# Layer 0's output projection: 48 fp32 steps replaced by three products of rounded parts each

## What is computed

```python
x = L0_attn_hidden_states
x = _layernorm(x + _L0_attn_ref(x, ...), axis=-1)
x = _layernorm(x + _L0_ffn_ref(x, L0_ffn_gate_w, L0_ffn_gate_up_proj, L0_ffn_down_proj), axis=-1)
x = _layernorm(x + _L1_attn_ref(x, ...), axis=-1)
x = _layernorm(x + _L1_ffn_ref(x, L1_ffn_weight, L1_ffn_bias), axis=-1)
```

```python
scores = jnp.einsum('bqhd,bkhd->bhqk', qf, kf) * scale      # 16 heads, causal
p = jax.nn.softmax(scores, axis=-1)
o = jnp.einsum('bhqk,bkhd->bqhd', p, v)
o = o.reshape(B, T, H * D_V) @ Wo                            # the output projection
...
logits = jnp.matmul(x.astype(jnp.float32), gate_w.T.astype(jnp.float32))
p = jax.nn.sigmoid(logits)
w, idx = jax.lax.top_k(p / jnp.sum(p, axis=-1, keepdims=True), TOPK)   # 2 of 16 experts a token
```

## Time and profile before

| | us |
|---|---|
| median of 3 runs | 534.26 (533.25 to 538.05) |
| the profiled execution | 533.59 |
| its span in the trace | 531.1 |
| TensorE busy | 497.8 |
| VectorE, ScalarE, GpSimd busy | 380.4, 339.7, 294.0 |

### The profile page before, as it was taken

One profiled execution on the slowest core, in us unless ns is written; L12 is line 12 of the kernel. 1 busy time (PEld: TensorE's weight loads), 2 busy tenths in 40 slices (PEclk: granted clock), 3 DMA queues, 4 the chain that ended last, 5 costly groups with the idle time before them and its releaser, 6 DMA issues.

```text
span 531.1 us, 10729 instructions
## 1 busy us (share of the span) xinstructions
PE 497.8 (94%) x3592; PEld 434.7 (82%) x3592; DVE 380.4 (72%) x833; ACT 339.7 (64%) x761; POOL 294.0 (55%) x289
## 2 busy tenths in 40 slices
PE   8999999999999996899958979999999999999994
PEld 7668888888888785688836869999999999999883
DVE  4798888888883275655537897779857985588556
ACT  5756777777766646344324776778766876676663
POOL 5757677767764136255551676776554664465330
PEclk9999999999999999899987988999999999999998
DMA  8939999940000672455564000000000000000001
GB/s 270 398 85 383 314 331 318 322 151 0 0 1 1 225 295 81 114 156 162 181 216 171 0 1 2 1 0 2 1 2 1 1 2 0 2 1 1 0 22 60
DMA packets 17756, 56.78 MB, mean 107 GB/s; under 512 B 2628, under 2 KB 12362, under 8 KB 15914
## 3 DMA queue, kind: packets, MB, share of 16 engines
q1 hardware_dynamic: 14960, 49.81, 27.5%
q0 software_dynamic: 2752, 6.40, 3.6%
HBM read 49.19 MB, written 28.45 MB: 146 GB/s over the span
## 4 chain that ended last, share of the span: by engine, by line
PE 78%; DVE 7%; ACT 5%; issue 3%; DMA 3%; POOL 2%; SPq 0%; DVEq 0%; POOLq 0%; ACTq 0%
PE bank L443 10%; PE bank L445 10%; PE bank L444 10%; PE bank L991 5%; PE bank L586 5%; PE bank L508 4%; PE bank L611 3%; PE bank L1008 3%; PE bank L588 2%; PE bank L735 2%; PE bank L720 2%; PE bank L722 2%; PE bank L721 2%; PE bank L622 2%; PE bank L702 2%
## 5 line engine op out<-in xcount | busy, mean ns | idle before, releaser
L1100 ACT ACTIVATE probs<-bank,neg_max,q_scale 128x256 f32<-128x256 f32 (+1 forms) x128 | 63.7, 507 | 39.1 <-DVE neg_max L1770 39.1
L1986 POOL TENSOR_TENSOR probs<-probs,inv_sum 128x512 f32<-128x512 f32 x64 | 51.5, 826 | 44.1 <-DVE inv_sum L1778 44.1
L2019 POOL TENSOR_TENSOR exps<-exps,tables 128x256 f32<-128x256 f32 x32 | 24.7, 771 | 75.2 <-ACT exps L1210 75.0
L1210 ACT ACTIVATE exps<-bank 128x768 f32<-128x768 f32 x32 | 25.9, 808 | 41.3 <-PE bank L702 41.3
L1590 DVE TENSOR_TENSOR q_lo<-q_sum,q_hi 128x512 fp32r<-128x512 f32 x32 | 28.8, 899 | 29.0 <-ACT q_hi L1164 28.6
L2006 POOL TENSOR_TENSOR swapped<-swapped,tables 128x512 f32<-128x512 f32 x32 | 43.4, 1359 | 5.2 <-ACT swapped L1131 5.1
L2115 POOL DMA_INDIRECT y_rows<-y_slot,dest x31 | 29.7, 959 | 30.0 <-issue 18.2
L1756 DVE TENSOR_TENSOR swapped<-bank,tables 32x512 f32<-32x512 f32 x64 | 44.4, 693 | 1.4
L1978 POOL TENSOR_TENSOR qT<-qT,swapped 128x512 f32<-128x512 f32 x32 | 40.8, 1274 | 6.1 <-DVE swapped L1756 6.1
L443 PE MATMUL bank<-x,wq_hi 128*128 128x256 f32 x128 | 38.6, 301 | 0.1
L586 PE MATMUL bank<-keysT,qT 128*128 128x256 f32 x128 | 38.2, 380 | 0.0
(11 more groups left out here) (281 smaller groups left out, 1766.6 us busy)
## 6 DMA issues: line engine op xcount, KB each, us to landing
slots<-in_c_unused SPq DMA_DIRECT2D x20, 1036.0 KB, 35.5
gu_all<-in_gate_up SPq DMA_DIRECT2D x4, 1024.0 KB, 7.8
xg<-slots SPq DMA_DIRECT2D x31, 129.5 KB, 2.2
wvo_raw<-in_wvo SPq DMA_DIRECT2D x1, 2560.0 KB, 18.4
dn_all<-in_down SPq DMA_DIRECT2D x1, 2048.0 KB, 7.7
wq_full<-in_Wq SPq DMA_DIRECT2D x1, 2048.0 KB, 17.8
wo_raw<-in_Wo SPq DMA_DIRECT2D x1, 2048.0 KB
wqk_raw<-in_wqk SPq DMA_DIRECT2D x1, 1536.0 KB, 9.9
```

The source lines that it names most:

```text
L1100: ins = act.activation(probs[:, par, h, c0:c1], bank[:, 2 * par + h, c0:c1], ACT.Exp, bias=neg_max[:, par, i:i + 1], scale=q_scale[:, b, t ...
L1986: ins = pool.tensor_tensor(some, some, inv, ALU.mult)
```

## The change

Tiles 2 to 7 are made as three products of parts (144 fp32r matmuls for 48 fp32 ones); tiles 0 and 1 stay. For this the parts are made:

- ScalarE makes the high part of `wo_full` in two halves of 4 pairs (128x1024 each) at the end of units 28 and 29, and the high part of `ctxT0` for batches 1, 2 and 3, two halves each: batch 1 at the end of units 30 and 31, batch 2 at the end of step 32 and in `act_first_norm` behind the sigmoid's table load of b = 0, batch 3 in b = 1, one ahead of the root and one behind the sigmoid's table load. `ctx0_hi` has room for two batches, so batch 3 waits until tile 3 is made.
- VectorE makes the low part of the weights in units 30 and 31, behind the reciprocal.
- GpSimd makes the low parts of the context, in place of `ctxT0`: batch 1 in units 30 and 31 behind the normalisation, batches 2 and 3 behind the last unit, ahead of the DMA of `triangles`.
- TensorE waits for the low parts (`o0["w_lo"]`, `o0["ctx_lo"]`) ahead of steps 0 and 4 of each batch's first tile, and no longer for `ctx_copied`.
- A few semaphores are shared by two uses each, to make room for the three new ones; no wait moves by that.

```diff
     def pe_out0(eng, t, i):
 
-        mm = eng.matmul(out_bank0(t), ctxT0[:, i, t * P:t * P + P], wo_full[:, i, :],
-                        start=i == 0 and t != 1, stop=i == PAIRS - 1, skip_group_check=True)
+        if t < 2:
+            mm = eng.matmul(out_bank0(t), ctxT0[:, i, t * P:t * P + P], wo_full[:, i, :],
+                            start=i == 0 and t != 1, stop=i == PAIRS - 1, skip_group_check=True)
+        else:
+            b, c0 = t // 2, t % 2 * P
+            if t % 2 == 0 and i % 4 == 0:
+                eng.wait_ge(o0["ctx_lo"], 2 * (b - 1) + i // 4 + 1)
+            mm = three_pass(eng, out_bank0(t), ctx0_hi[:, b % 2, i, c0:c0 + P],
+                            ctx0_lo[:, i, t * P:t * P + P], wo0_hi[:, i, :], wo0_lo[:, i, :],
+                            i == 0, i == PAIRS - 1)
...
-            eng.wait_ge(at0["ctx_copied"], 4 * (PAIRS - 1) + b + 1)
+            if t == 2:
+                eng.wait_ge(o0["w_lo"], 2)
...
             load_table(act, 2 * b + 1, ACT.Sqrt)
+            if b == 1:
+                act_context0_hi(act, 3, 0)
             act.wait_ge(ln["var_ready"], 2 * b + 2)
...
             load_table(act, 2 * b + 2, ACT.Sigmoid)
+            if b < 2:
+                act_context0_hi(act, b + 2, 1)
...
+    def act_context0_hi(act, b, half):
+
+        act.wait_ge(at0["ctx_copied"], 4 * (4 * half + 3) + b + 1)
+        if b == 2 and half == 0:
+            act.wait_ge(at0["scores_done"], 4 * PAIRS)
+        if b == 3 and half == 0:
+            act.wait_ge(ln["y_done"], 4)
+        act.activation(ctx0_hi[:, b % 2, some_pairs(half), :], ctxT0[:, some_pairs(half), T * b:T * b + T],
+                       ACT.Copy).then_inc(o0["hi"], 1)
+
+    def context0_lo(eng, b, half):
+
+        eng.wait_ge(o0["hi"], 2 * b + half + 1)
+        some = slice(T * b, T * b + T)
+        eng.tensor_tensor(ctx0_lo[:, some_pairs(half), some], ctxT0[:, some_pairs(half), some], raw(ctx0_hi[:, b % 2, some_pairs(half), :]),
+                          ALU.subtract).then_inc(o0["ctx_lo"], 1)
...
+            if isinstance(n, int) and n >= 4 * PAIRS - 4:
+                if n < 4 * PAIRS - 2:
+                    act_weights_out0_hi(act, n - 4 * PAIRS + 4)
+                elif n < 4 * PAIRS:
+                    act_context0_hi(act, 1, n - 4 * PAIRS + 2)
+                elif n == 4 * PAIRS:
+                    act_context0_hi(act, 2, 0)
...
+            if isinstance(n, int) and 4 * PAIRS - 2 <= n < 4 * PAIRS:
+                half = n - 4 * PAIRS + 2
+                dve.wait_ge(o0["hi"], half + 1)
+                dve.wait_ge(at["q_done"], 4 * PAIRS)
+                dve.tensor_tensor(wo0_lo[:, some_pairs(half), :], wo_full[:, some_pairs(half), :],
+                                  raw(wo0_hi[:, some_pairs(half), :]), ALU.subtract).then_inc(o0["w_lo"], 1)
...
             if own and ahead(p, b, more):
                 pool_sin(pool, at, *ahead(p, b, more))
+            if isinstance(n, int) and 4 * PAIRS - 2 <= n < 4 * PAIRS:
+                context0_lo(pool, 1, n - 4 * PAIRS + 2)
 
         steps(pool, body)
+        for b in (2, 3):
+            for half in range(2):
+                context0_lo(pool, b, half)
```

More of the change, by code:

```diff
@@ L149, in build @@
     q_minus = sb("q_minus", [P, B, 2])
+    with ExitStack() as out_parts:
+        ctx0_hi = sb("ctx0_hi", [P, 2, PAIRS, T], F32R, out_parts)
     with ExitStack() as blocks:
@@ L215, in build @@
         wa_raw = sb("wa_raw", [P, KD, PROJ], F32, setup)
+    with ExitStack() as lows:
+        ctx0_lo = sb("ctx0_lo", [P, PAIRS, B * T], F32R, lows)
     with ExitStack() as layer0:
@@ L277, in build @@
     wk_hi, wk_lo = w_hi, w_lo
+    wo0_hi = wo_hi[:, PAIRS:H, :]
+    wo0_lo = latT_lo[:].rearrange("p k n -> p (k n)").rearrange("p (g d) -> p g d", d=D)
     slots = nc.dram_tensor("slots", (REGIONS * REGION, W), F32, kind="Internal").ap()
@@ L473, in pe_logits @@
         if b == 0:
[L474 removed]
+            eng.wait_ge(mo["ids_ready"], 2)
         else:
```

34 lines of the change are left out of this document (19 added, 15 removed).

## The result

The changed kernel took 546.47 us, the median of four executions (545.61 to 547.47). The kernel before, measured beside it, took 533.94 (four, 533.25 to 538.05). The ratio is 1.0221, with a 95% interval of 1.0184 to 1.0258: slower by 12.5 us. The forecast was 543.0 with a range of 538.5 to 547.0. So the sign and the range were right, and the point was 3.5 us too low. The profiled execution took 547.47 us, 13.9 more than the profiled one of before, over a span of 545.7 us for 531.1; it is the slowest of the four.

The account below looks back on a forecast made before the run. TensorE was taken as the bound, busy 497.8 of 531.1 us. Terms: +9.2 us at the first prefix product, +0.4 after it, 0 in the tail, +9.6, taken as +9.4 on 533.6: 543.0 us, range 538.5 to 547.

Parts of the forecast that it names:

- The products: Projection, tiles 2 to 7: three products take 0.36 us against 0.444 per step, gaining 4.0 us at most.
- The wait: First prefix product waits for the triangles DMA behind four GpSimd subtractions, starting at 197.5, 9.2 us late.
- The early clock: Pause of about 2 us before the first routing product: no clock loss in the forecast, 1.3 us in rival 2.
- rival 2: Longer wait for the table: landing 2.2 us slower, early clock 1.3 us, or more; 545 to 549 us, chance 0.09.
- The length of the wait: TensorE, there at 189.1, stands still some 8.5 us before the first prefix product.
- VectorE beside GpSimd: GpSimd's last normalisation, beside VectorE's weights subtractions, late by 0 to 1.4 us, taken as 0.7.
- GpSimd's subtraction: Each 128x1024 context low part on GpSimd takes 2.5 us; 2.3 or, if stretched, 3.4 possible.
- After the wait: First prefix product to batch 2's routing product: 2.0 us gained, 2.4 lost at half clock, +0.4.
- The tail: From batch 2's routing product to the experts: 0 us change; scatters start at about 198 without further cost.
- Rival 1: TensorE's clock stays up or returns at once after the wait for the table: 540.6 us, chance 0.14.
- Rival 3: Table is there when TensorE needs it, so not slower: 533.1 us, or 529.6 with all gains; chance 0.07.

Follow-up runs that it names:

- e2: Changed kernel with 16 unused small matmuls on TensorE in the pause before the first routing product: 545.44 us, ratio 1.0201.
- e1: Changed kernel with the triangles DMA issued ahead of GpSimd's low parts of batches 2 and 3: 538.93 us, ratio 1.0075.
- e3: Kernel before, no new products or parts, with only the triangles DMA issued late, behind a wait and two GpSimd subtractions: 545.13 us, ratio 1.0181.
- e4: Changed kernel with VectorE's second weights low part held until GpSimd's last normalisation is done: 544.59 us, ratio 1.0180.
- e5: Changed kernel with ScalarE's two copies of layer 1's weights moved behind the copies of x of batches 0 and 1: 542.03 us, ratio 1.0128.
- e8: As e7, but VectorE makes batch 3's context low parts and layer 1's second weights low part goes behind batch 1's slots: 534.87 us, ratio 0.9988.
- e6: Changed kernel with both edits, of e1 (table first) and e5 (copies moved): 535.12 us, ratio 0.9993.
- e7: As e6, with VectorE's weights parts ahead of the last two reciprocals and GpSimd's context low parts behind the last normalisation: 534.03 us, ratio 0.9984.
- e6_again: The kernel of e6 unchanged, run in a later session: 537.07 us, ratio 1.0040.
- e7_again: The kernel of e7 unchanged, run in a second session on the same chip as e8: 538.57 us, ratio 1.0056.
- e7_third: The kernel of e7 unchanged, run a third time: 537.12 us, ratio 1.0046.
- e8_again: The kernel of e8 unchanged, run once more: 534.80 us, ratio 1.0003.

## Why the prediction was right, and where it was off

**The products.** Right: three starts cover 0.36 us where one fp32 step took 0.444. The 4.0 us were worked out right and, as the prediction said, the part before the first prefix product only lengthened the wait.

**The wait.** Right in its mechanism, its place, its releaser and every link but one, VectorE's addition of batch 1, which waited for the slowed steps of tile 3 and not for the choice of experts. The table's DMA was issued at 196.50 (prediction: 194.4 + 0.7 = 195.1) and the prefix product started at 198.99 (197.5): 10.8 us later than before, 0.36 of it start-up, where +9.2 was forecast. The 1.5 us between 197.5 and 198.99 come apart into 0.36 for the start-up, 1.06 for the early clock, 0.2 for the last normalisation, -0.25 for GpSimd's last subtraction and +0.2 for the table's landing; 191.8 + 0.1 + 2.5 + 2.3 is 196.7 and not 196.8, which takes 0.1 off.

**The early clock.** This is the step that failed, though the range had room for it. The prediction let the first pause, forecast at 2 us and 1.85 in the profile, pass at the full clock, though its own row had a fall after 1.58 us; it stood only in rival 2, at 1.3 us. The clock went to 0.58 in the first 2 us after the pause. The routing product took 1.49 us for 0.95, and three steps of tile 3 took 0.64 us each for the 0.36 reckoned. It entered the path twice, by the routing product and by the 0.45 us that VectorE's addition waited for tile 3. So the root of batch 1 came at 191.38, 1.7 us later than the 189.0 + 0.7 forecast, start-up and late normalisation included. e2 measured the clock's part at 1.06 us.

**The length of the wait.** 6.26 us against 8.5. TensorE was there at 192.7 and not at 189.1, and that is mostly the clock: eight steps at 0.64 us and the late routing product. A shorter wait was no saving, since it ended later. Forecasting the end of the wait was worth more than forecasting its length.

**VectorE beside GpSimd.** Mis-sized: 0.7 us was taken from a range of 0 to 1.4. The last normalisation lasted 0.91 us longer; that it began 0.43 later (173.22 for 172.79) is the start-up, as it started right behind its reciprocal in both. Tile 2 began 1.25 us later than before, 0.89 of it from this. The Trainium skill ("SBUF — State Buffer", "Who interferes with whom") has whole-instruction exclusion, by which the prediction put the delay nearer to 1.2 than to 0.7. The trace agrees with the exclusion: the subtraction that started first, at 173.06, kept its 1.21 us, and the normalisation that came in at 173.22 was held. The size is 0.91, what was left of the subtraction and not the whole of it.

**GpSimd's subtraction.** 2.34 to 2.38 us for an estimate of 2.5; a little in the other direction, which hid some of the early clock by luck.

**After the wait.** Forecast +0.4 between the prefix product and the routing product of batch 2. Measured: 12.6 us (198.99 to 211.63) for 12.5 before, +0.2 with the rounding of both. Half rate lasted until 203.4, 4.4 us after the wait for the 4.8 reckoned, so it cost 2.2 us against the 2.0 gained, and the clock had fallen during the wait, not after it.

**The tail.** Forecast 0, measured +1.1 us: the experts' first product came 21.6 us after the routing product of batch 2 and 20.5 before. Most of it, 0.9 us, lies behind the last prefix product, before VectorE reads its result (222.30, idle 1.16 us there and 0.24 before). No run tells why, and it does not go with the change: e2 has this pause too (1.15 us), e1, e3, e4 and e5 do not (0.22 to 0.24). The scatters, forecast at about 198, started at 200.65; the prediction's own rows put them 2.4 us behind the prefix product, near 200, and it cost nothing.

Behind the experts' first product the distance was 12.1 us there and 13.2 where TensorE goes on after its wait of 7.5 us for `yg` (280.10 before, 293.28 now). Then the clock was granted at 0.50 for longer:

```profile
293.28 4.00 PE L507 MATMUL bank<-alibi_keys 128*128 128x256 bf16 x18 [7.53 <-DMA yg<-y_rows]
...
305.50:306.00 0.50, 0.50 (x5) 0.50 (x4) 0.31 (x1) 0.49 (x2) 0.00 (x0) 0.71 0.00 0
```

It was back at about 305.8, 12.5 us after work began, for 4.8 before, and by then the distance was 16.0 us; it shrank to 14.6 at the end. Of the other profiles only that of e8 has so late a return, the others take 4 to 5 us, so it is not shown to belong to the change. The profiled execution is the slowest of the four, which fits.

**The sum by its terms**, in the profiled executions: 10.8 at the prefix product (10.5 without the start-up), +0.2, +1.1 in the tail, and 2.5 behind the experts' first product, the late clock above all; that is the 14.6 us between the spans, and 0.7 less lie outside the span. Forecast 9.2, 0.4, 0 and 0. By the medians the loss was 12.5 for 9.4 forecast, and the median of e3 with the wait alone was 10.1.

**The rivals.** Rival 1 (the clock stays up) is out: it fell twice. Rival 2 had the right term, the early clock, in about the right size (1.3 for 1.06); its other term, a landing slower by 2.2 us, did not come in the changed kernel (2.36 us for 2.3) but did in part in e5. Its 545 to 549 holds the measured 546.47 as the forecast's range does, so the time alone does not choose between them. Rival 3 set the price of the kernel at about nothing once the table is early, 0.5 us below the kernel before; e6 is that kernel with the two copies moved, at ratios of 0.9993 and 1.0040. Where the 4.0 us stay is seen in e6's first profile, counted from the last copy of ctxT: the routing product of batch 2 comes after 20.5 us for 23.1 in the kernel before, the experts' first product after 42.8 for 43.5. So 2.6 us arrive at the routing product, and 1.9 of them are given back behind it. Not on TensorE: from there to the last prefix product it takes 9.3 us in both, with the same waits for VectorE and ScalarE. From the last prefix product to the experts it is 12.96 us for 11.14. GpSimd's last scatter starts 6.0 us behind that product for 4.8, with no gap left in its queue behind the last low part, and its rows land after 3.3 us for 2.7. e8, which takes these low parts off GpSimd, starts its last scatter 1.1 us earlier than e7 and is not shown to be faster, so this bound is read from the traces and not proven by a run.

## What to carry to other kernels

Follow every instruction that an edit puts ahead of something in an in-order queue: here one 64 KB DMA behind four new subtractions cost most of 12.5 us, and a swap of lines gave 7.8 back, while of the 4 us of cheaper products 2.6 reached the routing product and 0.7 the experts. A part that is added in an idle stretch can still push back what its engine does last; here, by the traces, the scatters. Where an edit opens a pause in TensorE, reckon with half rate after it: a pause of 1.85 us was enough. Set two traces side by side from an instruction ahead of the change, and not from their starts. A difference under 1% between kernels of separate sessions is no result until one kernel has been run in both.

## What the runs showed of the hardware

**The clock.** A pause of 1.85 us was enough: granted 1.00 before it, 0.82 in the half microsecond from 186.0 and 0.50 (the 1.2 GHz level) from 186.5, with TensorE busy without a gap from 185.92. It came back at about 193.15 (0.85 in the half microsecond from 193.0), 7.2 us after work began, when TensorE had just stopped (192.73); it stood at 1.00 while TensorE was idle and fell again at about 196.6 (0.56 in the half microsecond from 196.5). In e1, with no second pause, it came back at about 195.0, 7.0 us after work began. After the long wait the return took 4.4 us, in e3 3.3. After the wait for `yg` it took 4.8 us before and 12.5 in the changed kernel's profile (e8: about 12). No run tells what sets this time.

**Eight elements, 2.35 us.** A VectorE copy of 128x8 took 0.16 us in the kernel before, 1.01 in the changed one beside a GpSimd normalisation, and 2.35 in e4 beside two GpSimd subtractions. A VectorE subtraction of 128x1024 took 3.24 us for 1.21 in e7.

The Trainium skill ("SBUF — State Buffer", "Who interferes with whom") tells this exclusion for a VectorE instruction with two SBUF inputs, and also lists the copy, whose one input is in SBUF here, among the operations that can contend with GpSimd. The trace agrees for both: the subtraction was held from 1.21 to 3.24 us, the copy from 0.16 to 2.35.

**Standstills with no releaser.** VectorE or ScalarE stood still for 3.2 to 5.0 us between 199 and 215 us in six of the profiles: e1 (ScalarE, at the copy of x of batch 2), e6_again (ScalarE, 3.71, at sigmoid), e7_again and e7_third (VectorE, both at L1458), e8 and e8_again (VectorE, both at L1970, 4.95 and 3.71). The same kernel had it at the same instruction, another kernel at another, and e6 and e7 had a session without it. The profile of the kernel before has none. What it is stays open. It may be a part of e1's loss of 0.75% and of the scatter below 1%; that was not separated.

The Trainium skill ("Runtime: NRT & Kernel Launch", "Instruction fetch mechanics") says that each engine fetches its instructions in blocks by DMA while it works. A block that comes late would stop one engine at a fixed instruction, as here. The traces rather speak against it: their queues of kind "instruction" show a transfer inside the standstill only in e6_again (201.0 to 201.5, 1.6 us before it ends) and none in the other five, and profiles without a standstill have such transfers too.
